# A gated recurrence and expert layer: the norm weight applied in the projection's copy, the gate product cut in halves, the residual copy on VectorE

## What is computed

```python
i = jnp.einsum('bld,ed->ble', x, Wi)
f = jnp.einsum('bld,ed->ble', x, Wf)
gate = jax.nn.sigmoid(f)
i_in = jax.nn.silu(i) * (1.0 - gate)
_, o = jax.lax.associative_scan(combine, (gate, i_in), axis=1)   # o[t] = gate[t]*o[t-1] + i_in[t]
g = jnp.einsum('bld,ed->ble', x, Wg)
rms = jax.lax.rsqrt(jnp.mean(jnp.square(g), axis=-1, keepdims=True) + EPS)
out = g * rms * g_norm_weight * (o * jax.nn.sigmoid(o))
return jnp.einsum('ble,de->bld', out, Wo)
```

## Time and profile before

| | |
|---|---|
| median of 2 runs | 4312.06 us (4311.77 to 4312.36) |
| the profiled execution | 4318.21 us |
| span of its slowest core, core 1 | 4316.7 us |
| spans of its cores | 4281.6 to 4316.7 us |
| TensorE matmuls busy | 3806.1 us (88%) |
| VectorE busy | 1332.6 us (31%) |
| ScalarE busy | 395.5 us (9%) |

### The profile page before, as it was taken

How to read it: one execution, slowest core, us unless ns; L and a number is a source line. 1 busy time by engine, 2 the same in 40 slices (tenths; PEclk the granted TensorE clock), 3 DMA queues, 4 the chain that set the end, 5 groups by cost and what they waited for, 6 DMA issues and landing times.

```text
span 4316.7 us, 43608 instructions; the slowest of 8 cores (4281.6 to 4316.7 us)
## 1 busy us (share of the span) xinstructions
PE 3806.1 (88%) x18832; PEld 1783.4 (41%) x18832; DVE 1332.6 (31%) x1122; ACT 395.5 (9%) x379; POOL 326.0 (8%) x358
## 2 busy tenths in 40 slices
PE   0998999979942699999999999999999999999992
PEld 0554444434422244444444444444444444444441
DVE  5322455542224222322322322322222232232233
ACT  3221111110032000000000000000000000000000
POOL 0000000000000000100100100000110010010011
PEclk9998999989965799999999999999999999999995
DMA  5113111102244343433443344234343343344239
GB/s 166 31 35 54 30 30 30 30 0 54 35 161 131 30 40 37 40 37 35 42 39 32 35 41 42 29 38 39 35 40 37 35 43 39 30 40 39 23 35 156
DMA packets 416189, 204.23 MB, mean 47 GB/s; under 512 B 399600, under 2 KB 399600, under 8 KB 407808
## 3 DMA queue, kind: packets, MB, share of 16 engines
q0 software_dynamic: 411216, 167.84, 32.2%
q1 hardware_dynamic: 4784, 33.61, 2.6%
HBM read 302.11 MB, written 33.55 MB: 78 GB/s over the span
## 4 chain that ended last, share of the span: by engine, by line
PE 80%; DVE 10%; DMA 6%; ACT 2%; issue 1%; DVEq 0%; POOL 0%; ACTq 0%; SPq 0%; POOLq 0%
PE pga L806 21%; PE pva L821 20%; PE pw L867 20%; PE po L565 5%; PE pg L327 5%; PE pi L467 3%; DMA y<-fsc 3%; PE pf L467 3%; DMA fsc<-x 2%; DVE fsc L497 2%; DVE fsc L504 1%; DVE fsc L494 1%; DVE fsc L505 1%; DVE bufA L252 1%; ACT fsc L501 1%
## 5 line engine op out<-in xcount | busy, mean ns | idle before, releaser
L806 PE MATMUL pga<-bufA,wsc 128*128 128x512 bf16 x4096 | 923.3, 384 | 12.4 <-DVE fsc L779 12.4
L867 PE MATMUL pw<-gvw,wsc 128*128 128x512 bf16 x4096 | 899.6, 383 | 21.5 <-DVE gvw L840 19.1
L821 PE MATMUL pva<-bufA,wsc 128*128 128x512 bf16 x4096 | 904.9, 379 | 0.0
L867 PEld LDWEIGHTS pw<-gvw,wsc 128*128 128x128 bf16 x4096 | 403.1, 99 | 518.0 <-issue 46.2
L806 PEld LDWEIGHTS pga<-bufA,wsc 128*128 128x128 bf16 x4096 | 404.5, 99 | 512.4 <-issue 41.5
L821 PEld LDWEIGHTS pva<-bufA,wsc 128*128 128x128 bf16 x4096 | 400.9, 98 | 483.2
L741 POOL DMA_DIRECT2D wsc<-w x256 | 258.1, 1009 | 2532.1 <-PE pga L806 1199.4
L879 DVE TENSOR_TENSOR bufB<-pw,bufB 128x1024 bf16<-128x1024 f32 x224 | 274.3, 1225 | 525.4 <-PE pw L867 525.4
L833 DVE TENSOR_TENSOR gvw<-fsc,pga 128x1024 bf16<-128x1024 f32 x128 | 156.3, 1221 | 814.5 <-ACT fsc L829 814.5
L829 ACT ACTIVATE fsc<-pga 128x1024 f32<-128x1024 f32 x128 | 131.1, 1024 | 2519.9 <-PE pga L806 2519.9
L837 DVE TENSOR_TENSOR scr<-pva,fsc 128x1024 bf16<-128x1024 f32 x128 | 156.7, 1224 | 577.3 <-PE pva L821 577.3
(11 more groups left out here) (110 smaller groups left out, 1379.5 us busy)
## 6 DMA issues: line engine op xcount, KB each, us to landing
wsc<-w POOLq DMA_DIRECT2D x128, 512.0 KB, 6.6
fsc<-x SPq DMA_DIRECT2D x32, 1024.0 KB, 6.6
y<-fsc POOLq DMA_DIRECT2D x32, 1024.0 KB, 9.1
wsc<-w POOLq DMA_DIRECT2D x128, 256.0 KB, 4.6
wsc<-wg POOLq DMA_DIRECT2D x16, 512.0 KB, 5.7
wsc<-wo POOLq DMA_DIRECT2D x16, 512.0 KB, 5.1
gvw<-wi POOLq DMA_DIRECT2D x16, 512.0 KB, 6.1
gvw<-wf POOLq DMA_DIRECT2D x16, 512.0 KB, 7.3
```

The lines of the kernel that those rows point to most:

```text
L806: ins = e.matmul(out=pga[:, n2 * 512:(n2 + 1) * 512], lhsT=lhsT, rhs=bufA[:, k * 2048 + nn:k * 2048 + nn + 512], start=(k == 0), stop=(k = ...
L821: ins = e.matmul(out=pva[:, n2 * 512:(n2 + 1) * 512], lhsT=lhsT, rhs=bufA[:, k * 2048 + nn:k * 2048 + nn + 512], start=(k == 0), stop=(k = ...
L867: ins = e.matmul(out=pws[_sl][:, n2 * 512:(n2 + 1) * 512], lhsT=lhsT, rhs=gvw[:, k * 2048 + nn:k * 2048 + nn + 512], start=(k == 0), stop= ...
```

## The change

Three edits. In the projection stage L335 scales by `gwt` while it copies g, one factor per partition, after a wait for the load of `gwt`; the square L338 still reads the unscaled PSUM. In the input and gate stage the (gate - 1) * bX product is made per half, right after each sigmoid of f, so that the first half stands on VectorE's queue before the copies L435; and the last two operations become one multiply by bufB, into bufB. In the residual stage the copy with its sum moves from ScalarE to VectorE, as a `tensor_scalar` (times 1, plus 0) with an accumulator, behind L607; ScalarE's square waits for it, and so does the next load into the buffer.

```diff
--- before.py
+++ after.py
@@ -332,9 +332,10 @@
                     vmm = emit("tensor", gmm, inc=te)
                     mm_last[m] = vmm
                     wait("scalar", te, vmm)
+                    wait("scalar", miscg, MISC_G)
                     emit("scalar", lambda e, _m=m, _h=h: e.activation(
                         out=bufB[:, _m * 2048 + _h * 1024:_m * 2048 + _h * 1024 + 1024],
-                        in_=pgs[_h][:], func=AF.Copy), inc=ac)
+                        in_=pgs[_h][:], func=AF.Copy, scale=gwt[:, _m:_m + 1]), inc=ac)
                     pg_rel[h] = emit("scalar", lambda e, _m=m, _h=h: e.activation(
                         out=gsqb[_m % 2][:, _h * 1024:_h * 1024 + 1024],
                         in_=pgs[_h][:], func=AF.Square), inc=ac)
@@ -487,13 +488,15 @@
                             pf_rel = emit("scalar", lambda e, _h=h: e.activation(
                                 out=bGate[:, _h * 1024:_h * 1024 + 1024], in_=pf[:],
                                 func=AF.Sigmoid), inc=ac)
+                            wait("vector", ac, pf_rel)
+                            emit("vector", lambda e, _h=h: e.scalar_tensor_tensor(
+                                out=bX[:, _h * 1024:_h * 1024 + 1024],
+                                in0=bGate[:, _h * 1024:_h * 1024 + 1024], scalar=1.0,
+                                in1=bX[:, _h * 1024:_h * 1024 + 1024],
+                                op0=ALU.subtract, op1=ALU.mult))
                     if h == 0 and m + 1 < TEm:
                         if_prep(m + 1)
 
-                wait("vector", ac, pf_rel)
-                emit("vector", lambda e: e.scalar_tensor_tensor(
-                    out=bX, in0=bGate, scalar=1.0, in1=bX,
-                    op0=ALU.subtract, op1=ALU.mult))
                 v_scan = emit("vector", lambda e: e.tensor_tensor_scan(
                     out=bX, data0=bGate, data1=bX, initial=0.0,
                     op0=ALU.mult, op1=ALU.subtract), inc=ve)
@@ -502,11 +505,9 @@
                     out=bGate, in_=bX, func=AF.Sigmoid), inc=ac)
                 wait("vector", ac, a_sw)
                 emit("vector", lambda e: e.tensor_tensor(out=bX, in0=bX, in1=bGate, op=ALU.mult))
-                emit("vector", lambda e, _m=m: e.tensor_tensor(
-                    out=bX, in0=bX, in1=bufB[:, _m * 2048:(_m + 1) * 2048], op=ALU.mult))
-                wait("vector", miscg, MISC_G)
-                u_ev = emit("vector", lambda e, _m=m: e.tensor_scalar_mul(
-                    bufB[:, _m * 2048:(_m + 1) * 2048], bX, gwt[:, _m:_m + 1]), inc=ve)
+                u_ev = emit("vector", lambda e, _m=m: e.tensor_tensor(
+                    out=bufB[:, _m * 2048:(_m + 1) * 2048], in0=bX,
+                    in1=bufB[:, _m * 2048:(_m + 1) * 2048], op=ALU.mult), inc=ve)
         TE_B = te.n
         xs.rel[0] = [(ve, ve.n)]
         xs.rel[1] = [(ve, ve.n)]
@@ -611,14 +612,14 @@
                 wait("gpsimd", ve, v_r)
                 spl = spill.load(lambda e, _i=i, _t=t: e.dma_start(
                     out=yout[_t * 128:(_t + 1) * 128, :], in_=xs_ap[_i]))
-                wait("scalar", ve, v_r)
-                v_cp = emit("scalar", lambda e, _i=i, _t=t: e.activation(
-                    out=bufB[:, _t * 2048:(_t + 1) * 2048], in_=xs_ap[_i], func=AF.Copy,
-                    accum_out=st1(SUM, _t)), inc=ac)
+                v_cp = emit("vector", lambda e, _i=i, _t=t: e.tensor_scalar(
+                    bufB[:, _t * 2048:(_t + 1) * 2048], xs_ap[_i], 1.0, 0.0,
+                    ALU.mult, ALU.add, accum_out=st1(SUM, _t)), inc=ve)
+                wait("scalar", ve, v_cp)
                 emit("scalar", lambda e, _t=t: e.activation(
                     out=gvw[:, 0:2048], in_=bufB[:, _t * 2048:(_t + 1) * 2048],
                     func=AF.Square, accum_out=st1(SQ, _t)), inc=ac)
-                xs.release(slot, [(ac, v_cp), (spl[1], spl[2])])
+                xs.release(slot, [(ve, v_cp), (spl[1], spl[2])])
 
         v_inv2 = batch_invstd()
```

## The result

| | before | after |
|---|---|---|
| median | 4312.06 us | 4257.47 us |
| the profiled execution | 4318.21 us | 4257.47 us |
| span of its slowest core | 4316.7 us (core 1) | 4255.9 us (core 3) |
| spans of its cores | 4281.6 to 4316.7 | 4237.3 to 4255.9 |

The ratio is 0.9868, 95% interval [0.9855, 0.9882]: 1.3% faster and inside the range. The forecast of 4248 is missed by 9.5 us by that median, and by 7 by the ratio (0.9868 of 4312 is 4255).

What follows compares the result with a forecast made beforehand. TensorE was taken as the bound, waiting on a VectorE/ScalarE chain and losing clock in the gate stage. 39.5 + 26.0 - 0.4 - 1 = 64.1 us off 4318.2 gave 4254, median 4248; range 4232 to 4274.

Steps and rivals of the forecast that it cites:

- The chain: Gate stage: VectorE/ScalarE work that TensorE waits for gets 2.47 us shorter a turn, 16 times, saving 39.5 us.
- The clock: Gate stage i groups: with 1.12 us idle TensorE keeps 2.4 GHz, so 26.0 us of half-clock loss come back.
- rival 1: Gate stage: the clock still falls after 1.12 us idle, a group losing about 1.7 us; 4272 us, chance 0.11.
- Scale on L335: Projection stage: multiplying by gwt during ScalarE's copy costs 0, any growth (about 93 ns by the skill) being hidden.
- The residual stage: Moving the copy to VectorE spreads tiles on all cores; costs 1 us at the start, 0.4 at the end.
- the bound of 4: Residual stage: upper bound, in us, on the cost of the spread start, whose bounds were 0 to 4.
- a sign of being wrong: Residual stage: the prediction would be wrong if the slowest core's stage grew by more than 4 us.
- +1: Residual stage start: 1 us put in the sum; core 1 loses at most 1.3 us for each first few tiles.
- the step from 4254 to 4248: Whole kernel: from forecast execution to forecast median, because the median of runs was 6.1 us below the profiled execution.
- rival 3: Gate stage: the merged multiply runs at L508's rate, gaining 1.0 us more a turn, 16 in all; 4232 us, chance 0.05.
- an end under 4225.8: Whole kernel: faster by over 2%, needing rival 3 and no idle time left as well; chance 0.05.

Runs made afterwards that it cites:

- gate_stage_only: The whole change with the residual stage's copy and sum back on ScalarE, so only the gate stage edits and the L335 scale; 4244.8 us, one execution.
- gate_stage_only2: Second run of the whole change with the residual copy back on ScalarE; 4233.2 to 4242.9 us, ratio 0.9843 [0.9821, 0.9865].
- whole_again: The whole change measured once more, on the same chip as gate_stage_only2; 4251.3 to 4256.7 us, ratio 0.9880 [0.9851, 0.9908].
- residual_only: The kernel before with only the residual stage's copy and sum moved to VectorE; 4316.3 us, one execution.
- the ten: Ten executions of the unchanged kernel before, on the chip of residual_only; 4303.6 to 4313.2 us, mean 4307.6.
- pairs_act: gate_stage_only plus a wait: each even residual tile's load also waits for the preceding odd tile's store; 4236.6 to 4239.4 us, ratio 0.9841 [0.9819, 0.9864].
- merge_only: The kernel before with only L505 and L508 made one and the scale on L335, L494 whole; 4268 to 4280 us, ratio 0.9908 [0.9876, 0.9941].
- split_only: The kernel before with only L494 cut in halves; 4271 to 4284 us, ratio 0.9923 [0.9897, 0.9949].

## Why the prediction was right

*The chain, 39.5 us.* Right in each term: L494's half 1.23 (taken 1.22), the merged multiply 2.29 (2.29), idle time 1.13 (1.12), 2.92 (2.90) and 14.47 (14.4). The copies behind the first half cost nothing.

*The clock, 26.0 us.* Right: 30.9 us became 4.5. The stage gained 65.0 us between the slowest cores, and 65.5 was the forecast. But the reading behind it was thinner than its result. I placed 1.12 between 0.83 (no loss) and 2.34 (loss) as if a limit lay there; the runs show a share of turns with a fall that grows from 0 of 14 at 1.13 us over 8 at 2.19 and 11 at 2.52 to 14 at 3.59. That 1.13 us lies where nothing is lost was in part luck: no row between 0.83 and 2.34 us spoke for it. What rival 1 priced does not happen at 1.13 us and would have been about half as dear at 2.2.

*Scale on L335.* Nothing on the path, as priced: the projection stage took 270.7 to 276.7 us by core, before 272.6 to 276.4. ScalarE's groups after (the copy is L336 now) show what one costs:

```profile
L336 ACT ACTIVATE bufB<-pg,gwt 128x1024 bf16<-128x1024 f32 x32 | 35.6, 1114 | 224.7 <-PE pg L327 224.7
```

It takes 1114 ns where it took 1024, 90 ns more, hidden beside a group of 6.91 us. The Trainium skill ("ScalarE: Activation LUTs", on what an ACTIVATE costs) has about 93 ns for the pointer operand, and the trace agrees.

*The residual stage, 1.4 us.* This is the term that was mis-sized. Its mechanism was right: 4.9 us of distance, all eight cores spread, 9.2 us a tile, the store's issue at 0.53, the copy at 2.29. Between the two slowest cores it cost 4.7 us up to the last L608, over the bound of 4 and over the 4 us that I had named as a sign of being wrong, and 1.6 behind it, where I had 0.4. The step that failed is that +1 was worked out for core 1 alone, as the core that would end last. Core 1 lost 2.9 us. Core 3, for which the prediction has no price, lost 20.1 and became the slowest; core 6 lost 28.1 and ended 12 us before it, as forecast. Before, a core was late only if its own tiles had spread; after, each has.

By the ratios of kernels with and without the edit it costs 11 to 16 us, nearer to the mean core's 13.0 (and 18.3 against gate_stage_only) than to the slowest core's 4.7. The spans of all cores bear this out on the new kernel: from gate_stage_only2 to whole_again, three executions each, the mean core goes from 4225.0 to 4241.6 us and the slowest from 4237.0 to 4251.8. On the kernel before it is less: the mean core loses 15 us, the slowest 9 (residual_only, one execution, against the ten).

*The base and the sum.* The forecast for the execution was 4318.2 - 64.1 = 4254, and that execution's counterpart took 4257.5, 3.4 us more. The residual stage took 4.9 us more than its term and the gate stage gave 0.5 less; 2.0 came back in the stages for which nothing was forecast (1.0 of it in the output projection). Part of the small error is thus luck. The other 6.1 us of the 9.5 are the step from 4254 to 4248. It rested on the profiled execution before, which lay 6 us over its median; the one after lay within 2 us of what the ratio gives, so that carrying the distance over was not justified.

*The chances.* They do not fit together: rival 3 has 0.05 at 4232, inside the range, and an end under 4225.8, which needs rival 3 and more, has 0.05 as well.

Open: the residual edit cost some 8 us on the kernel before (one execution) and 11 to 16 on the new one; whether these differ isn't told apart. Nor did a run show why a store beside a load takes 8.6 us and one beside a store mostly under 5.

## What to carry to other kernels

A chain on other engines that ends on TensorE costs its idle time and, beside that, the clock's fall; shortening it paid twice here until the idle time was near 1 us, each piece by itself too. With two buffers that are each stored and loaded again, the phase between them decides how long their transfers take: work put between the two producers may cost nothing on its own engine and yet shift that phase on every core. When cores differ, price an edit by what it does to all of them, not only to the slowest: another may end last.

## What the runs showed of the hardware that I had not expected

- The same idle time before the same work brings TensorE's clock down in some turns and not in others: 2.19 us in 8 of 14, 2.52 us in 11 of 14. Where it fell in the turns of this table (core 3 of merge_only, core 0 of split_only), a group of 32 lost 1.68 us (8.75 against 7.07); behind 3.59 us it lost 1.3 to 3.0.
- A store of 1 MB took 4.4 to 6.8 us beside another store (pairs_act, core 4) and 8.1 to 8.8 beside a load (after, core 3). With all eight cores in pairs they take 115 to 121 us for the stage, the fastest single ones among spread cores 104 to 107.
- A VectorE copy of 2048 f32 columns without an accumulator, 1.23 us, holds POOL's store issue until it ends (0.90 us for 0.53); with one, 2.29 us, it does not.
